# Products with v in four runs of two sets per batch, and a new table of slots

## The reference

```
h = relu(layernorm(x))
# block 1: attention, 8 heads of 16
q, k, v = h @ W_qkv + b_qkv                       # per head
y = softmax(where(adj, q @ k.T / 4, -inf)) @ v    # 512 x 512 scores per head
x = x + y @ W_out + b_out
# block 2: two kernels over the 512 nodes
h = relu(layernorm(x)); z_l = h @ Wl; z_g = h @ Wg
A_l = max(zn @ zn.T, 0), zn = z_l / |z_l|                      # "cos"
A_g = exp(-|z_g[i] - z_g[j]|^2 / 2)                            # "rbf"
K = 0.9 * rows_to_one(A_l * adj) + 0.1 * rows_to_one(A_g * adj)  # without the diagonal
x = x + (K @ (h @ Wv)) @ Wo
```

## Time and profile before

| | |
|---|---|
| time, median of 3 runs | 874.0 us (873.55 to 875.01) |
| the profiled execution | 872.33 us, span 870.6 us, granted clock 0.988 |
| TensorE busy | 814.5 us (94%), 4860 products |
| VectorE busy | 674.6 us (77%) |
| ScalarE busy | 544.3 us (63%) |
| GpSimd busy | 532.0 us (61%) |
| products with v (L708) | 1024, 138.1 us busy |
| probability masks on GpSimd (L547) | 256, 322.4 us |

### The profile page before, as it was taken

The page is one execution under the profiler, slowest core; times in us unless marked ns, Lnnn a source line. Parts: engine busy times, 40 slices in busy tenths (PEclk is TensorE's granted clock), DMA queues, the critical chain, the costliest instruction groups (busy, mean ns, idle before and its releaser), DMA issues.

```text
span 870.6 us, 15444 instructions
## 1 busy us (share of the span) xinstructions
PE 814.5 (94%) x4860; PEld 467.4 (54%) x4860; DVE 674.6 (77%) x1950; ACT 544.3 (63%) x1230; POOL 532.0 (61%) x701
## 2 busy tenths in 40 slices
PE   3869899999999999999999999999999999999986
PEld 2223245646564655656565564656556565646466
DVE  5666669798887969788796978878797888878266
ACT  5427485765758485665848566574957657474832
POOL 4266766675857567585756658575665757474611
PEclk9899899999999999999999999999999999999999
DMA  3350505032140503113050402304050221300000
GB/s 94 100 138 3 141 1 141 1 102 53 43 111 1 152 2 114 41 58 96 5 148 2 141 13 78 76 22 132 2 153 2 85 69 36 106 2 13 13 1 25
DMA packets 49840, 54.75 MB, mean 63 GB/s; under 512 B 7264, under 2 KB 43616, under 8 KB 49760
## 3 DMA queue, kind: packets, MB, share of 16 engines
q1 hardware_dynamic: 49760, 53.76, 22.5%
HBM read 30.28 MB, written 23.07 MB: 61 GB/s over the span
## 4 chain that ended last, share of the span: by engine, by line
PE 54%; DVE 16%; POOL 11%; issue 7%; ACT 6%; DMA 3%; SPq 2%; POOLq 0%; DVEq 0%; ACTq 0%
PE adj L722 12%; PE pv L708 9%; PE score L680 7%; PE turned L694 7%; DVE scrap L955 6%; PE adj L717 6%; PE work L740 4%; PE turned L693 4%; POOL probs_t L547 3%; DVE adj_cos L974 3%; DVE adj_rbf L988 3%; DVE rbf_arg L983 2%; PE work L717 2%; POOL v_cos L632 2%; POOL v_cos L629 2%
## 5 line engine op out<-in xcount | busy, mean ns | idle before, releaser
L547 POOL TENSOR_TENSOR probs_t<-probs_t,keep_t 128x512 int32<-128x512 int32 x256 | 322.4, 1280 | 213.4 <-ACT probs_t L1126 213.1
L955 DVE CUSTOM_DVE_ANT_0 scrap<-score,mask_add 128x512 f32<-128x512 f32 x512 | 340.0, 683 | 67.6 <-PE score L680 65.3
L1126 ACT ACTIVATE probs_t<-turned 128x512 f32<-128x512 f32 x512 | 296.2, 601 | 110.5 <-PE turned L694 105.1
L680 PE MATMUL score<-qk_rows 96*128 96x512 bf16 x512 | 198.9, 388 | 12.1 <-DMA qk_rows<-k_dram 6.0
L694 PE MATMUL turned<-qk_rows 99*128 99x512 bf16 x512 | 196.2, 383 | 9.7 <-ACT probs_t L1126 8.8
L708 PE MATMUL pv<-probs_t,v_cols 128*32 128x512 f32 x1024 | 138.1, 612 | 0.0
L680 PEld LDWEIGHTS score<-qk_rows 96*128 96x128 bf16 x512 | 49.9, 98 | 119.8 <-DVE neg_max L955 55.2
L693 PE MATMUL turned<-bar_t,ident_b 128*128 128x512 bf16 x256 | 98.0, 383 | 0.7 <-ACT probs_t L1126 0.7
L694 PEld LDWEIGHTS turned<-qk_rows 99*128 99x128 bf16 x512 | 50.6, 99 | 54.7 <-ACT probs_t L1126 18.3
L1160 ACT ACTIVATE rbf_exp<-rbf_arg,rbf_bias 128x512 f32<-128x512 f32 x64 | 46.2, 722 | 34.7 <-DVE rbf_arg L983 32.8
L722 PEld LDWEIGHTS adj<-v_cos,adj_cos 128*128 128x128 f32 x480 | 62.8, 191 | 8.8 <-DVE out_sb L1011 0.6
(11 more groups left out here) (159 smaller groups left out, 1221.9 us busy)
## 6 DMA issues: line engine op xcount, KB each, us to landing
q_dram<-split SPq DMA_DIRECT2D x96, 128.0 KB
qk_rows<-q_dram SPq DMA_DIRECT2D x32, 384.0 KB, 4.3
k_dram<-split SPq DMA_DIRECT2D x48, 128.0 KB
qk_rows<-k_dram SPq DMA_DIRECT2D x32, 192.0 KB, 4.8
x_sb<-in_x_dram SPq DMA_DIRECT2D x16, 256.0 KB, 4.2
qk_rows<-k_dram SPq DMA_DIRECT2D x32, 128.0 KB, 4.9
out_dram<-out_sb SPq DMA_DIRECT2D x15, 256.0 KB, 2.5
qk_rows<-k_dram SPq DMA_DIRECT2D x32, 64.0 KB, 5.2
```

What stands on the lines that cost most here:

```text
L547: pool.tensor_tensor(tile, tile, keep_t[:, w // HG % T, :], ALU.mult).then_inc(probs_masked.sem, 1)
L680: pe.matmul(score_bank[u % 2][:, :], qk_rows[0:ROWS, b % 2, 0, h, t * P:(t + 1) * P], qk_rows[0:ROWS, b % 2, 1, h, :], start=True, stop=Tr ...
L955: dve.tensor_tensor_reduce(scrap[:, u % 2, :], score_bank[u % 2][:, :], mask_add[:, u % T, :], -1.0, 3.0e38, ALU.add, ALU.min, neg_max[:, ...
L1126: act.activation(probs_t[:, k % 4, w % HG, :], turned_bank[w % 2][:, :], ACT.Exp, scale=SCALE).then_inc(probs_ready.sem, 1)
```

## The change

`attend` takes a pair of sets: it waits for all eight tiles of both, and for v and the bank if it is the first pair of a group, then issues the four products of the one set and the four of the other. The signal per set stays. The stage "pv" has four slots (32, 40, 48, 56) for eight (28, 32, ... 56). Many other entries of `AT` move, mostly by one or two slots; AT_BEFORE_LAST and AT_LAST are unchanged. On SyncE the order of the stages stays as it is though their numbers change. Among the moves in the steady pattern (slots modulo 32): z 2 and 3 from 8 and 9 to 9 and 10, pv_copy of the first group from 10 to 14 on ScalarE, y of the first group from 22 to 20, v and v_add from 19 to 18, cos_read 2 from 21 to 24 and rbf_read 3 from 23 to 25 on VectorE, mix_cos and mix_rbf 1 from 31 to 0 and mix_rbf 3 from 1 to 4, q_split from 12 to 8, x_biased from 19 to 15 and k_split from 20 to 19 on GpSimd.

```diff
--- before.py
+++ after.py
@@ -41,24 +41,24 @@
 
 AT = {
 
-    "hT": (-26,), "q": (-24,), "k": (-22,), "v": (-13,), "max_turn": (17, 32),
-    "pv": (28, 32, 36, 40, 44, 48, 52, 56), "y": (54, 59), "yT": (60,), "attn": (62,), "h2T": (66,),
-    "z": (69, 71, 72, 73), "zgT": (76,), "col": (78,), "zlT": (79,), "rbf": (79, 83, 85, 87),
-    "cos": (81, 83, 84, 90), "mix_cos": (92, 95, 96, 97), "mix_rbf": (94, 95, 96, 97),
-
-    "ln_scale": (-28,), "hT_copy": (-26,), "q_hi": (-24,), "k_hi": (-22,), "max_copy": (17, 31),
-    "pv_copy": (42, 56), "yT_copy": (60,), "ln2_scale": (64,), "h2T_hi": (66,), "z_copy": (70, 71, 72, 74),
-    "z_sums": (71, 72, 74, 75), "zgT_hi": (75,), "col_copy": (77,), "zlT_hi": (79,), "rbf_exp": (82, 83, 86, 90),
-
-    "ln_moments": (-36,), "hT_split": (-26,), "q_rest": (-24,), "k_rest": (-21,), "v_add": (-13,),
-    "max_split": (13, 30), "y_scale": (57, 59), "x1": (62,), "ln2_moments": (63,), "h2T_lo": (67,),
-    "zgT_lo": (76,), "zlT_lo": (79,), "rbf_read": (80, 83, 85, 87), "cos_read": (81, 83, 85, 90),
-    "rbf_mask": (83, 84, 88, 92), "out": (94, 96, 97, 101),
-
-    "ln_rstd": (-32,), "q_split": (-20,), "k_split": (-12,), "x_biased": (-13,), "ln2_rstd": (62,),
-    "z_norms": (76,),
-
-    "qk_store": (-12,), "rows": (-6, -4), "x_next": (-9,), "max_load": (-2, 29), "store": (95,),
+    "hT": (-27,), "q": (-24,), "k": (-22,), "v": (-14,), "max_turn": (17, 32), "pv": (32, 40, 48, 56),
+    "y": (52, 58), "yT": (60,), "attn": (62,), "h2T": (67,), "z": (69, 71, 73, 74), "zgT": (76,), "col": (78,),
+    "zlT": (79,), "rbf": (79, 83, 85, 87), "cos": (81, 83, 84, 89), "mix_cos": (92, 96, 97, 98),
+    "mix_rbf": (94, 96, 97, 100),
+
+    "ln_scale": (-30,), "hT_copy": (-26,), "q_hi": (-24,), "k_hi": (-22,), "max_copy": (16, 31),
+    "pv_copy": (46, 56), "yT_copy": (60,), "ln2_scale": (65,), "h2T_hi": (66,), "z_copy": (69, 71, 73, 74),
+    "z_sums": (70, 71, 74, 75), "zgT_hi": (75,), "col_copy": (77,), "zlT_hi": (78,), "rbf_exp": (81, 83, 86, 90),
+
+    "ln_moments": (-36,), "hT_split": (-26,), "q_rest": (-24,), "k_rest": (-22,), "v_add": (-14,),
+    "max_split": (13, 30), "y_scale": (56, 58), "x1": (63,), "ln2_moments": (63,), "h2T_lo": (68,),
+    "zgT_lo": (77,), "zlT_lo": (78,), "rbf_read": (78, 83, 85, 89), "cos_read": (82, 83, 88, 90),
+    "rbf_mask": (83, 84, 88, 92), "out": (95, 96, 97, 101),
+
+    "ln_rstd": (-31,), "q_split": (-24,), "k_split": (-13,), "x_biased": (-17,), "ln2_rstd": (63,),
+    "z_norms": (75,),
+
+    "qk_store": (-21,), "rows": (-8, -7), "x_next": (-21,), "max_load": (-5, 26), "store": (95,),
 }
 
 AT_BEFORE_LAST = {
@@ -695,20 +695,23 @@
                           qk_rows[0:ROWS + 3, b % 2, 0, h, :], start=w not in by_pe,
                           stop=True).then_inc(turned_filled.sem, 1)
 
-            def attend(b, k):
-                g, j = divmod(k, T)
-                ends = (k + 1) * HG
+            def attend(b, pair):
+
+                g = 2 * pair // T
+                ends = 2 * (pair + 1) * HG
                 reached(pe, probs_masked, b, sum(w < ends for w in by_pool))
                 if by_pe:
                     reached(pe, probs_ready, b, 1 + max(w for w in by_pe if w < ends))
-                if j == 0:
+                if 2 * pair % T == 0:
                     reached(pe, v_ready, b)
                     reached(pe, pv_copied, b, g)
-                for hl in range(HG):
-                    last = pe.matmul(pv_bank[32 * hl:32 * (hl + 1), :], v_cols[:, b % 3, j, g * HG + hl, :],
-                                     probs_t[:, k % 4, hl, :], start=(j == 0), stop=(j == T - 1),
-                                     tile_position=(0, 32 * hl))
-                last.then_inc(pv_filled.sem, 1)
+                for k in (2 * pair, 2 * pair + 1):
+                    j = k % T
+                    for hl in range(HG):
+                        last = pe.matmul(pv_bank[32 * hl:32 * (hl + 1), :], v_cols[:, b % 3, j, g * HG + hl, :],
+                                         probs_t[:, k % 4, hl, :], start=(j == 0), stop=(j == T - 1),
+                                         tile_position=(0, 32 * hl))
+                    last.then_inc(pv_filled.sem, 1)
 
             def split_product(dst, left, right, before_rest=None):
                 for part, (a, c) in enumerate(((0, 0), (0, 1), (1, 0))):
```

## The result

The changed kernel takes 878.3 us (median of 5 runs, 877.7 to 880.2) against 874.0: 1.005 of before (95% interval 1.0037 to 1.0062), slower by 0.5%. Forecast was 865.1, in 860 to 880 with 0.24 for slower. The steady period did not shorten by 0.59 us, it grew by 0.10.

A forecast was written before the change was run, and what follows sets the result against it. TensorE's own stream was taken as the bound, 48.6 of 50.14 us per batch. Terms -0.68 + 0.32 - 0.13 - 0.1 = -0.59, times 13 = -7.7, plus -1.2 elsewhere, gave -8.9: 865.1 us, range 860 to 880.

The forecast's parts named there:

- runs of the v products: TensorE's eight v-product runs per batch become four, saving 0.17 us for each set: -0.68 us a batch.
- k product waits for q's rest: No such wait forecast (0); the walk of TensorE and ScalarE started at the k product.
- T25: Turned product of tile 25, waiting on ScalarE's exp of tile 23: stall grows from 0.72 to 1.04 us, +0.32 a batch.
- S22, S23, last rbf product: TensorE behind VectorE's masks: S23 loses 0.5 us against 0.63 lost at the last rbf product; scattered 0.1 also goes.
- The seam: Distance between the two sets inside a paired run: taken as 0.46 us, bounds 0.46 and 0.62.
- Waits of the pair itself: A paired run's first instruction waits for eight tiles instead of four on TensorE; costed at nothing.
- dead heat: First rbf mask on VectorE (8.65 us after zlT) against GpSimd's M29 (8.6); forecast let the rbf mask in first.
- rival (a): GpSimd's M29 holds off the first rbf mask; S22 and S23 lose 2.1 us; +1.0 a batch, 886 us; chance 0.20.
- the third rbf product: On TensorE, it lost 0.63 us waiting for VectorE's bank read; forecast to find its bank read.
- SyncE: Next batch's row load becomes just due, 19.0 to 19.5 us after max_turn0; costs nothing but caps better results.
- The fill: Three half-filled or tail batches, where only the v-product runs count: 3 x -0.4 = -1.2 us.
- (b): Stalls take most of the gain through mask, seam or row load: 0.3 to 0.6 us a batch back, 869 to 873; chance 0.20.

The follow-up runs named there:

- the kernel with the split: Kernel before with only SyncE's order changed: q's stores and k's first store issued ahead of the load of the row maxima; 862.5 us (0.987).

## Why the prediction was wrong

The balance of one steady period, each line by its own rows (the losses by the usual distance of two starts):

| step | predicted | measured |
|---|---|---|
| runs of the v products | -0.68 | -0.91 (4 x 0.23) |
| k product waits for q's rest | 0 | +0.45 |
| T25 and the score product before it | +0.32 | +0.17 |
| S22, S23, last rbf product | -0.23 | +0.28 |
| elsewhere | 0 | +0.11 |
| sum | -0.59 | +0.10 |

**Runs.** Right in kind, the size too small. The seam costs nothing: the starts inside the run are 0.45, 0.43 and 0.43 apart, so the later parts are even 0.03 nearer than the first distance that was taken for all three. No load of 0.11 us shows at the seam, though the tiles share all rows: the second set's first loads start at 425.64, together with the products of the first set's second part and 0.43 ahead of their own. That a weight load overlaps a running product only when its row group differs, as the Trainium skill says (TensorE: Matmul & The Clock Gate, packing small matmuls), does not describe this trace.

**Waits of the pair itself.** Right: none in the steady periods. Between a turned product and the next work a pair takes 2.16 to 2.17 us in all of them.

**The k product, the step that was missing (0 forecast, +0.45 measured).** The prediction walked TensorE and ScalarE from the k product's start and took that start as given. Ahead of it lies the same hand-over of the work bank, with VectorE's rest of q, and before it was exactly due (2.59 us from q to k, 2.58 now that k waits). The z product that "enters there" (0.53) has left from between q and k, where it was the cover of that hand-over: it was booked where it came in and not where it went out. Putting it back only moves the wait to zgT, as the run showed. The walk began one product too late.

**T25.** Right in kind, half the size (+0.32 forecast, +0.17 measured). From the k product to T25 4.74 us (4.85 forecast), of which TensorE's own 3.85 (3.81 forecast): 0.89 lost where 1.04 was forecast.

**Masks against GpSimd, the other step that failed (-0.23 forecast, +0.28 measured).** This was called a dead heat and given to the rbf mask. M29 was first, by 0.17 us: rival (a)'s trigger. Its second half did not follow, as the second mask got ahead of the subtraction by 20 ns, so 1.10 of (a)'s 2.1 us came, about half. No row of before showed a probability mask against an rbf mask; the rows of after do (1.67), and in the run with the third pair joined the subtraction alone does it. All of them agree with the rule of the Trainium skill (SBUF — State Buffer, who interferes with whom), an exclusive lock in order of arrival, int32 masks included. A dead heat of 0.05 us at the end of a walk of 8.6 us is open to both sides; 0.50 for the one and 0.20 for the other was more than the walk could tell. (What the prediction calls the third rbf product is rbf3, the last of four.)

**SyncE.** Just due, as forecast: rows land 0.2 us ahead of S0 (460.69, 460.87). They land 19.9 behind the turn of the first maxima (440.81), where 19.0 to 19.5 was given; the prediction's own rows span 18.5 to 19.8. It did not decide in this kernel, since the period never got short enough.

**The fill.** Costed at -1.2 with the tail, by the runs alone; in the profiled executions the first three periods grew by 4.7 instead. It was read as half empty and therefore harmless, but in it S0's wait for its rows adds to the length, and the clock makes it dearer.

**The sum.** The range (to 880) held the time, the forecast did not. That the range held it is luck: no case of the prediction ends there ((b) at 873, (a) at 886), and the right one was a mixture of (a) and an overlooked wait. The general fault: what a run covers in the slot that it leaves was walked for slots 12 and 20 only, for slot 12 from one product too late, and for slots 28 and 4 not at all. The runs with one pair each show, in before's slots, that three of the four were cover; in the changed kernel the moved transposes of h show no wait, so there the cover of slot 4 cost nothing.

## What to carry to other kernels

Where one engine is full, a piece of its work that can be put anywhere is the cover of some other engine's chain; before it is joined or moved, list for each place it leaves which hand-over starts ahead of it and ends behind it, and walk from the product that fills the shared bank, not from the next one. A wait that is due to lost time of a second engine (here VectorE held off by GpSimd) goes only if that time is given back; moving the waiting step moves the wait. And look at the fill apart from the steady part: one order of transfers on SyncE was worth 11.6 us there, more than the whole change was meant to bring; with the bias addition moved and the first pair joined the kernel takes 851.4 us.

## What was unexpected of the hardware

- Which engine pays for the collision is decided by tens of nanoseconds: at 20 ns ahead an rbf mask takes 0.68 and GpSimd's subtraction 1.68; 0.04 us behind the subtraction the mask took 1.67.
- A GpSimd conversion with one input (CAST, 0.62 us) holds the mask off as well (1.04 when it came 0.13 us behind).
- A late row load can cost twice: a wait of 2.64 us was followed by products at the lower clock (0.61 for 0.39), and the stretch of that batch shows 0.95 where the kernel with the split, after 1.28, shows 1.00.
- Further sets in one run of four-column-group products cost 0.43 us per part, with no gap of entry or exit between sets.
